# A cross network and tower on one core: tiles stored in three parts, and the next unit's first layer computed later in a slot

## What is computed

```python
e = jnp.stack([tbl_0[ids[:, 0]], ..., tbl_23[ids[:, 23]]], axis=1)      # 1024 x 24 x 16
for W in (W0, W1, W2):                                                  # 64 outputs each
    Xk = jnp.einsum('bfd,bhd,fho->bod', X0, Xk, W.reshape(24, H_prev, 64))
    outs.append(Xk.sum(axis=2))
h = jnp.concatenate([*outs, dense_ctx], axis=1)                         # 1024 x 208
h = jnp.maximum(h @ W_top1 + b_top1, 0.0)
h = jnp.maximum(h @ W_top2 + b_top2, 0.0)
y = h @ W_top3
```

## Time and profile before

| what | value |
|---|---|
| runs | 423.68, 424.27, 428.24 us; median 424.27 us |
| profiled execution | 421.92 us |
| its span, first to last instruction | 420.1 us |
| TensorE matmuls | 342.1 us busy (81%) |
| VectorE | 288.5 us (69%) |
| ScalarE | 189.7 us (45%) |
| POOL | 233.2 us (55%), last gather issued at 298.6 us |
| DMA queue of SP | 53090 packets, 71.66 MB, 74.2% of 16 engines |

### The profile page before, as it was taken

One profiled execution on the slowest core, in us unless ns is written; L12 is line 12 of the kernel. 1 busy time (PEld: TensorE's weight loads), 2 busy tenths in 40 slices (PEclk: granted clock), 3 DMA queues, 4 the chain that ended last, 5 costly groups with the idle time before them and its releaser, 6 DMA issues.

```text
span 420.1 us, 6106 instructions
## 1 busy us (share of the span) xinstructions
PE 342.1 (81%) x2296; PEld 150.5 (36%) x2296; DVE 288.5 (69%) x277; ACT 189.7 (45%) x346; POOL 233.2 (55%) x252
## 2 busy tenths in 40 slices
PE   0045899438396969599999997999999999999997
PEld 0043422102041323244333433543444344443466
DVE  2001499129385959578987998798899999898700
ACT  1000026113335345273737573757556475745374
POOL 5775888888888888788788887677400000000000
PEclk9998899859886999999999999999999999999999
DMA  3355936499799998999799979998999799731000
GB/s 101 74 111 116 231 83 157 83 231 234 164 242 233 252 257 152 228 231 213 163 228 223 232 137 222 233 235 163 225 251 266 156 251 258 214 107 44 2 2 2
DMA packets 59263, 73.63 MB, mean 175 GB/s; under 512 B 31489, under 2 KB 36609, under 8 KB 59234
## 3 DMA queue, kind: packets, MB, share of 16 engines
q1 hardware_dynamic: 53090, 71.66, 74.2%
q0 software_dynamic: 6144, 1.59, 3.2%
HBM read 48.05 MB, written 1.58 MB: 118 GB/s over the span
## 4 chain that ended last, share of the span: by engine, by line
PE 68%; DMA 10%; issue 9%; POOL 3%; another core or an unknown queue 2%; ACT 2%; SPq 2%; DVE 1%; DVEq 0%; ACTq 0%
PE ps_x L370 44%; PE ps_tower L370 9%; PE ps_turn L370 6%; PE ps_b L370 5%; POOL x_rows L191 3%; DMA A<-x_scratch 3%; DMA B_sb<-x_sb 2%; DMA x_scratch<-x_rows 2%; PE ps_turn L415 2%; PE ps_turn L423 1%; SPq L256 1%; DMA C<-x_scratch 1%; DVE Z L337 1%; PE ps_tower L376 1%
## 5 line engine op out<-in xcount | busy, mean ns | idle before, releaser
L347 DVE TENSOR_TENSOR Z<-A,ps_b 128x1024 f32<-128x1024 f32 x192 | 222.0, 1214 | 29.5 <-remote 18.8
L191 POOL DMA_INDIRECT x_rows<-tbl,ids_sb x192 | 190.8, 994 | 62.6 <-issue 43.6
L370 PE MATMUL ps_x<-Z,w_sb 128*64 128x512 f32 x768 | 188.4, 609 | 1.7 <-issue 1.0
L337 DVE TENSOR_TENSOR Z<-A,C 128x1024 f32<-128x1024 f32 x48 | 58.1, 1224 | 75.5 <-DMA C<-x_scratch 37.4
L370 PEld LDWEIGHTS ps_x<-Z,w_sb 128*64 128x64 f32 x768 | 50.3, 139 | 84.3 <-issue 65.8
L370 PE MATMUL ps_x<-Z,w0s_sb 128*64 128x512 f32 x192 | 48.3, 626 | 24.4 <-DVE Z L337 23.9
L635 ACT ACTIVATE x_diag<-ps_turn,mask_sb 128x192 f32<-128x192 f32 x128 | 50.6, 606 | 9.9 <-PE ps_turn L423 9.8
L618 ACT COPY ps_b<-B_sb 128x1024 f32<-128x1024 f32 x45 | 46.4, 1030 | 9.8 <-DMA B_sb<-x_sb 5.9
L648 ACT COPY G<-ps_turn 128x416 f32<-128x416 f32 x31 | 15.7, 506 | 73.5 <-remote 45.8
L599 ACT COPY x_sb<-ps_x 128x512 f32<-128x512 f32 x16 | 9.4, 586 | 78.2 <-PE ps_x L370 78.2
L204 POOL MEMSET pause_sb<- 128x768 f32 x56 | 42.3, 756 | 3.6 <-DMA x_scratch<-x_rows 3.6
(11 more groups left out here) (48 smaller groups left out, 147.2 us busy)
## 6 DMA issues: line engine op xcount, KB each, us to landing
A<-x_scratch SPq DMA_DIRECT2D x48, 512.0 KB
B_sb<-x_sb SPq DMA_DIRECT2D x90, 256.0 KB
C<-x_scratch SPq DMA_DIRECT2D x32, 512.0 KB
x_rows<-tbl,ids_sb POOLq DMA_INDIRECT x192
x_quarters<-x_scratch SPq DMA_DIRECT2D x16, 96.0 KB
x_scratch<-x_rows SPq DMA_DIRECT2D x7, 192.0 KB
w_sb<-w SPq DMA_DIRECT2D x2, 384.0 KB
C<-x_scratch SPq DMA_DIRECT2D x2, 256.0 KB
```

What stands on the lines that cost most here:

```text
L191: pool.indirect_dma_start(out=x0_rows[t % 2][:, f * D:(f + 1) * D], out_offset=None, in_=tables[f], in_offset=bass.IndirectOffsetOnAxis(ap ...
L337: nc.vector.tensor_tensor(Z[s % ZR][:, :], A[u % AS][i][:, :], C[u % 2][i][:, :], ALU.mult).then_inc(z_ready, 1)
L347: nc.vector.tensor_tensor(Z[s % ZR][:, :], A[u % AS][i][:, :], ps_b[j % 2][:, :], ALU.mult)\
L370: return nc.tensor.matmul(out, lhsT, rhs, start=start, stop=stop)
```

## The change

- A tile is stored to the scratch in three parts of 8 fields (`store_part`), each when its 8 gathers have landed. Tile A0 of the tile's first unit is loaded behind part 0, C0 and A1 behind part 1, C1 and A2 behind part 2; SP waits for each part's store to land. The second unit's loads follow, and B of either unit stands between.
- POOL pauses after each gather by a memset of 288 columns (before: of 768 after three), and no longer waits for VectorE; it waits for the store of the same part of the tile two back.
- `x1_at`: the first layer of unit u+1 stands ahead of product 9 in slots 2 to 14 and behind product 11 in slot 1.
- `copy_c` is split: its first half stands ahead of `spread_x0(u)`, its second half behind, both for unit u+1 (before: both ahead of it, for unit u+2). `copy_x1(u+1)` moves behind it and behind the dense layers' copies. `make_b` moves from product 7 to product 10, and three of the tower's pieces to the front of a slot.
- All dense weights (1.4 MB in 8 DMAs) are loaded at the start, not in slot 3.

```diff
-PAUSE = 768
+PAUSE = 288
...
-BURST = 3
+BURST = 1
...
-    return NP2 // 2 if u < 2 else 0
+    return 6 if u == 0 else NP2 if u == 1 else 9
...
             for f in range(F):
-                gather(0, f, gathered_part[f // FR])
-            pool.wait_ge(part_stored[NI - 1], 16)
...
             for t in range(1, TILES):
-                if t >= 2:
-                    wait_stored(pool, t - 2)
                 for f in range(F):
+                    if t >= 2 and f % FR == 0:
+                        wait_stored(pool, t - 2, f // FR)
                     if f % BURST == 0:
                         pool.memset(pause_sb[:, :], 0.0).then_inc(paused, 1)
                         pool.wait_ge(paused, (F * (t - 1) + f) // BURST + 1)
-
-                    after(pool, z_ready, PER_SLOT * (2 * t - 5) + 2 * PER_SLOT * f // F)
-                    gather(t, f, gathered[t % 2])
+                    gather(t, f, part_gathered[t % 2][f // FR])
...
+            for dst, src in ((w2_sb[:, :, :], w2), (wt1a_sb[:, :], wt1[0]), (wt1b_sb[:, :], wt1[1]),
+                             (wt2_sb[:, :, :], wt2), (wt3_sb[:, :], wt3), (bt1_sb[:, :], bt1),
+                             (bt2_sb[:, :], bt2), (dense_sb[:, :], dense_t)):
+                sp.dma_start(dst, src).then_inc(tower_in, 16)
+            def store_part(t, i):
+                sp.wait_ge(part_gathered[t % 2][i], 16 * FR * (t // 2 + 1))
+                v = x0_dram[t:t + 1, FR * i:FR * (i + 1), :].rearrange("t f (b d) -> (t b) f d", d=D)
+                src = x0_rows[t % 2][:, D * FR * i:D * FR * (i + 1)].rearrange("p (f d) -> p f d", d=D)
+                sp.dma_start(v, src).then_inc(part_stored[t % 2][i], 16)
...
-            for u in range(2, UNITS):
-
-                if u == 2:
+            def free_a(u, i):
+
+                if u >= AS:
+                    sp.wait_ge(z_ready, made_x2(u - AS, NP2 - NI + i))
+
+            def free_c(u):
+                sp.wait_ge(z_ready, made_x1(u - 2, NI - 1))
+
+            for t in range(TILES):
+                u = 2 * t
+                if t > 0:
+
+                    free_c(u + 1)
+                    for i in range(NI - 1):
+                        load_c(u + 1, i)
                     for k in range(NJ - 1):
-                        load_b(u - 1, k)
-                    store_tile(1)
-                if u % 2 == 0:
-                    wait_stored(sp, u // 2)
-                sp.wait_ge(z_ready, made_x1(u - 2, NI - 1))
-                for i in range(NI - 1):
-                    load_c(u, i)
-                for i in range(NI):
-                    if u >= AS:
-                        sp.wait_ge(z_ready, made_x2(u - AS, NP2 - NI + i))
-                    load_a(u, i)
-                if u > 2:
+                        load_b(u, k)
+                    for i in range(NI):
+                        free_a(u + 1, i)
+                        load_a(u + 1, i)
+                    for e in range(2):
+                        sp.wait_ge(x0_turned, u + e - 1)
+                        load_quarters(u + e)
+                if t + 1 < TILES:
+
+                    store_part(t + 1, 0)
+                    if t == 0:
+                        for k in range(NJ - 1):
+                            load_b(1, k)
+                    store_part(t + 1, 1)
+                    wait_stored(sp, t + 1, 0)
+                    free_a(u + 2, 0)
+                    load_a(u + 2, 0)
+                    if t > 0:
+                        for k in range(NJ - 1):
+                            load_b(u + 1, k)
+                    wait_stored(sp, t + 1, 1)
+                    free_c(u + 2)
+                    load_c(u + 2, 0)
+                    free_a(u + 2, 1)
+                    load_a(u + 2, 1)
+
+                    store_part(t + 1, 2)
+                    wait_stored(sp, t + 1, 2)
+                    load_c(u + 2, 1)
+                    free_a(u + 2, 2)
+                    load_a(u + 2, 2)
+                else:
                     for k in range(NJ - 1):
-                        load_b(u - 1, k)
-                if u % 2 == 1 and u + 1 < UNITS:
-                    store_tile((u + 1) // 2)
-                sp.wait_ge(x0_turned, u - 1)
-                load_quarters(u)
-                if u == W - 1:
-                    for dst, src in ((w2_sb[:, :, :], w2), (wt1a_sb[:, :], wt1[0]), (wt1b_sb[:, :], wt1[1]),
-                                     (wt2_sb[:, :, :], wt2), (wt3_sb[:, :], wt3), (bt1_sb[:, :], bt1),
-                                     (bt2_sb[:, :], bt2), (dense_sb[:, :], dense_t)):
-                        sp.dma_start(dst, src).then_inc(tower_in, 16)
-            for k in range(NJ - 1):
-                load_b(UNITS - 1, k)
+                        load_b(u + 1, k)
...
-                for n in range(NP2):
+                for n in range(NP2 + 1):
                     if n == x1_at(u) and u + 1 < UNITS:
                         for i in range(NI):
                             cross1(u + 1, i)
-                    cross2(u, n)
-                    if n == x1_at(u) + 4 and u + 1 < UNITS:
-                        sum_x1(u + 1)
+                    if n < NP2:
+                        cross2(u, n)
+                    if n == 1 and u > 0:
+                        sum_x1(u)
...
-                if w == 0 and n in (8, 9, 10):
-                    at = 4 * (n - 8)
+                if w == 0 and n in (6, 8, 9):
-                if w == 1 and n in (1, 5, 8):
-                    sum_h1(g, (1, 5, 8).index(n))
-                if (w, n) == (2, 1):
+                if w == 1 and n in (-1, 5, 8):
-                if (w, n) == (3, 1):
+                if (w, n) == (3, -1):
...
+                if g > 0:
+
+                    tower(g - 1, w, -1)
...
                         turn_x0(u)
-                        if u + 1 < UNITS:
-                            make_b(u + 1, 0)
+                    if n == (7 if u == 0 else 10) and u != 1 and u + 1 < UNITS:
+                        make_b(u + 1, 0)
...
+                if u == 1:
+                    turn_x2(u)
+                    for i in range(NI):
+                        cross1(u + 1, i)
+                    make_b(u + 1, 0)
...
-            def copy_c(u):
-
-                for i in range(NI - 1):
-                    act.wait_ge(C_in[u % 2][i], 16 * uses(u))
+            def copy_c(u, i):
+
+                act.wait_ge(C_in[u % 2][i], 16 * uses(u))
                 if u >= 2:
                     act.wait_ge(z_ready, made_x1(u - 2, NI - 1))
                 c = C[u % 2]
-                nc.scalar.copy(c[NI - 1][0:64, :], c[1][64:128, :]).then_inc(c_copied, 1)
-                nc.scalar.copy(c[NI - 1][64:128, :], c[0][0:64, :]).then_inc(c_copied, 1)
+                if i == 0:
+                    nc.scalar.copy(c[NI - 1][64:128, :], c[0][0:64, :]).then_inc(c_copied, 1)
+                else:
+                    nc.scalar.copy(c[NI - 1][0:64, :], c[1][64:128, :]).then_inc(c_copied, 1)
...
                 if u > 0:
                     copy_x2(u - 1)
-                if 2 <= u < UNITS - 1:
-                    copy_x1(u + 1)
+                    copy_x2_rows(u - 1)
+                if u == 2:
+                    copy_x1(2)
+                    copy_b(2, 0)
                 if u > 0:
-                    copy_x2_rows(u - 1)
...
-                if u == 1:
-                    copy_c(2)
-                if u < 2:
-                    copy_x1(u + 1)
-                elif u + 2 < UNITS:
-                    copy_c(u + 2)
+                if 0 < u < UNITS - 1:
+                    copy_c(u + 1, 0)
+                if u == 0:
+                    copy_x1(1)
                 if towers and w == 0:
                     copy_z12(g - 1)
                 if towers and w == 1:
                     relu_h1(g - 1, 1)
                 spread_x0(u)
+                if 0 < u < UNITS - 1:
+                    copy_c(u + 1, 1)
...
-                if u + 1 < UNITS:
+                if 1 < u < UNITS - 1:
+                    copy_x1(u + 1)
+                if u != 1 and u + 1 < UNITS:
                     copy_b(u + 1, 0)
```

More of the change, by code:

```diff
@@ L128, in cin_tower @@
         ids_in = sem("ids_in")
-        gathered_part = [sem(f"gathered_part{i}") for i in range(NI)]
-        gathered = [sem(f"gathered{p}") for p in range(2)]
-        part_stored = [sem(f"part_stored{i}") for i in range(NI)]
-        x0_stored = [sem(f"x0_stored{p}") for p in range(2)]
+        part_gathered = [[sem(f"part_gathered{p}{i}") for i in range(NI)] for p in range(2)]
+        part_stored = [[sem(f"part_stored{p}{i}") for i in range(NI)] for p in range(2)]
         ident_in, mask_in, pick_in, w0_in, w1_in, tower_in = (sem(n) for n in (
@@ L175, in after, with wait_stored @@
                 engine.wait_ge(semaphore, count)
-        def wait_stored(engine, t):
-            if t == 0:
-                for i in range(NI):
-                    engine.wait_ge(part_stored[i], 16)
-            else:
```

(31 more changed lines are left out.)

11 lines of the change are left out of this document (6 added, 5 removed).

## The result

The changed kernel takes 470.57 us (median of 4 runs, 463.07 to 478.40); the kernel before took 424.92 (4 runs). The ratio is 1.108, 95% interval 1.099 to 1.116: 11% slower. Forecast were 450 us and a range of 430 to 472. The profiled execution took 472.05 us, the second slowest of the four; its span is 470.2.

The account below looks back on a forecast made before the run. Before, TensorE bound the steady part; after, a loop from x1 to x1 would. 88 + 207.7 + 90.8 + 18.3 + 16.6 gave 421.4, plus 24.5 a span of 446, 450 us as median; range 430 to 472.

Parts of the forecast that it names:

- full lateness of `sum_g`: Rival: `sum_g` results stay as late as before while POOL gathers, 40 us in full, giving 466 us; chance 0.27.
- to x1 of unit 11 (gathering): Slots 2 to 10 while POOL gathers: 207.7 us of loops, plus 24.5 for late `sum_g` or data waits.
- to x1 of unit 15: Slots 11 to 14, without gathers: 4 x 21.6 + 3.5 + 0.9 = 90.8 us.
- to the end: Slot 15 at 18.3 us, then 16.6 us from the last product to the end, as before.
- Part 1: The start: tile 1 stored in parts puts x1 of unit 2 at 88, its product 0 at 89, 24 us earlier.
- Part 2: Slots from 2 on: each x1 leads to the next through engines in turn, 21.6 us, 22.1 while POOL gathers.
- The data terms: Slots while POOL gathers: quarters and the last A come late from the DMA queue, 1 us a slot, 9 in all.
- Lateness of `sum_g`: Term while POOL gathers: 18 x 2.2 = 40 us in full, hiding the 9 of data waits; middle of both taken, 24.5.
- the bare loop: Slots 2 to 10 with neither late `sum_g` nor data waits: 207.7 us.
- Clock: Rival: TensorE's idle spells bring half clock in each of 9 early slots, about 3 us each, giving 477; chance 0.05.
- The faster rival: The loop does not bind, all as before from product 0 of unit 2 at 89; median 400 us; chance 0.08.
- The sign that was named for the loop: First-layer products of i = 2 wait on ScalarE's copy of C for 2 to 3 us in every slot from 3 on.

Follow-up runs that it names:

- `x2_first`: The changed kernel with `copy_x2(u-1)` ahead of `copy_b(u, 0)` on ScalarE from slot 3 on; 1.108 of the kernel before.
- `after_nogather`: The changed kernel without the gathers and pauses of tiles 2 to 7, so its output differs; 460.8 us, 1.115 of the kernel before.
- `start_alone`: The kernel before with only the change's start: tile 1 in three parts, unit 2's loads between, dense weights first, first layer moved up to slot 3; 430.6 us, 1.012.
- `before_burst1`: The kernel before with only the change's POOL pauses, 288 columns after each gather instead of 768 after three; 419.1 us, 0.978.

## Why the forecast came out as it did

The range held the time and the direction was right; the value was 20 us short, and 470.57 is only 1.4 us inside the range, two of the four executions outside it. The rival whose number comes nearest, full lateness of `sum_g` (466), is not what happened: the lateness was small, and terms that the sum had too short made up for it. Its sum against the profiled span, by the copies of x1:

| stretch | forecast | measured |
|---|---|---|
| start to x1 of unit 2 | 88 | 97.3 |
| to x1 of unit 11 (gathering) | 207.7 + 24.5 | 237.3 |
| to x1 of unit 15 | 90.8 | 98.9 |
| to the end | 34.9 | 36.7 |
| sum | 446 | 470.2 |

**Part 1** was right in kind (product 0 of unit 2 15 us earlier, not 24) and 9.3 us off in size. Among the signs of being wrong stood x1 of unit 2 not before 95; it was there at 97.3, so by that sign this part failed, in three steps. SP issued C1 and A2 at 84.2 and 84.7, not 80.3. The third product started at 91.73 and not 4.6 us behind the issue, since `copy_c` (88.82 to 89.86) and A2 stood between. And the copy of x1 came 5.0 us behind it, not 2.1:

```profile
90.40 1.12 PE L430 MATMUL ps_turn<-id_sb,x_sb 128*128 128x128 f32 x4 [6.23 <-ACT x_sb L647]
91.44 5.19 PE L385 MATMUL ps_x<-Z,w0s_sb 128*64 128x512 f32 x12
```

`turn_x2(1)` is ahead of the first layer on TensorE and waited for a ScalarE copy that stood behind `copy_c`; all 12 matmuls were left for the end, at 1.2 GHz behind 6.2 us of idling.

**Part 2**, the loop, was the right mechanism with its order of steps, and its own size was nearly right; I missed what runs beside it. The copies of x1 behind 300 us are 23.5 to 26.1 us apart (21.5 to 22 said, 25 where w = 0). Legs behind 320 us: x1 to `turn_x2` 5.9 (5.0 said: B lands for `copy_b` 4.2 us behind the copy, not 3.3), to the end of `turn_x0` 9.5 in slots 11 and 15 (9.4 said), to the copy of x1 7.4 in slots 13 and 14 (7.2 said), but 8.2 in slot 11, where the last A comes last, and 9.9 in slot 12 (w = 0). The data terms were in the sum, but as 1 us a slot and only while POOL gathers. Quarters came about 16.5 us behind x1, not 15.4, and the last A 20.5 to 23, not 20, behind 300 us too. That the data come so close behind the engines that cutting the loop alone gives little was nowhere in the forecast.

**Lateness of `sum_g`**: I took the middle of 9 and 40, 24.5. It was 10.4 us between 100 and 300 us, near the lower end. The gathering slots were 29.6 over the bare loop, which the 24.5 comes near by luck, since other reasons fill it: data (slot 7 had 11.5 us in its last leg, for C1 and A) and the clock. The kernel before with the single pauses has half the lateness; `x2_first`, with the same pauses, has 31.6. So pauses are one factor of at least two, and the chip is another.

**Clock**, given 0.05, was partly true. TensorE ran about 52 us at 1.2 GHz where it had been 20, and 24.7 us more busy time stand in the page. In slots 3, 5 and 9, which hold such stretches, the middle leg took 12.4 to 13.1 us, against 9.5 in slots 7, 11 and 15; in slots 5 and 9 part of that is dense work (slot 9 of `after_nogather`, at full clock, has 10.3). The Trainium skill (TensorE: Matmul & The Clock Gate, "Part 1: The HAM clock gate") holds idleness to be what halves the clock; the rows below agree. Idleness in sum does not tell it, though: behind 320 us TensorE idles as large a share as over the whole, and the clock is 0.99. I had argued that spells of 2 to 3 us are too short to do it. The rows show two of them, in slots 3 and 9, each with half clock behind it (127 to 134 and 291 to 294 us):

```profile
127.56 1.11 PE L430 MATMUL ps_turn<-id_sb,x_sb 128*128 128x128 f32 x4 [2.44 <-issue]
...
289.48 0.66 PE L430 MATMUL ps_turn<-id_sb,x_sb 128*128 128x128 f32 x4 [3.57 <-ACT x_sb L647]
```

The clock came on top of the loops and was no case of its own: its 32 us more at half rate are worth at most 16 us of full-rate work, a third of the 50 us.

**The faster rival** needed a mean slot under 22.9 us; it was 26.0 ((436.3 - 98.5) / 13). The sign that was named for the loop showed in part: VectorE did wait for the copy of C, by name 5 times between 97 and 440 us (20.6 us), not in every slot. The reasoning that 24 us of the start are given back in the loop alone was too narrow, though: `start_alone` gives the start back with no loop at all, at tile 2.

**A version that is faster than both**: `before_burst1`, 2.2% below before (1.1 to 3.3%). It is one line pair of this change.

## What to carry to other kernels

When work is moved so that its result is used as soon as it is made, write down every chain that leads from one result to the next, through each engine's order and through each issuing queue, and take the longest; where two lie close together, curing one gives only the distance to the other. An in-order queue that stands for a result before it issues one transfer delays all transfers behind it, and those may feed the next result (here C1 18.4 and the last A 20.5 us behind x1). An earlier start is only worth what the next supply, here tile 2's gathers and loads, lets through. And a control should run beside its own baseline on the same chip: one without gathers on one chip says little of a lateness seen on another.
